# A two-layer graph network: the first layer's sums mapped to values head by head, and branch numbers loaded at other places

## The chip, the cores and the metric

The kernel runs on one core of one Trainium2 chip. The metric is the device time of one execution in microseconds (us). PE is TensorE (PEld its weight loads), DVE is VectorE, ACT is ScalarE, POOL is GpSimd, SP is SyncE. All data are float32.

## What is computed

6250 nodes with 160 features (64 scalars, 32 vectors of three components) and 200,000 edges, sorted by their target node `dst`, pass two message layers. Each layer starts with a layer norm and a relu. Cut to what matters:

```python
# layer 0, for every edge, H = 4 heads
msg = (norm(node) @ W_src)[src] + (norm(node) @ W_dst)[dst]
m1 = tensor_product(msg, y, rbf @ W_rbf)
a = leaky(m1_s @ W_alpha).reshape(e, H, 16) . alpha_dot           # one logit a head
ex = exp(a - segment_max(a, dst)[dst]);  den = segment_sum(ex, dst)
m2 = tensor_product(sigmoid(m1_s @ Ws_val), m1_v @ Wv_val * gate, y, w2)
h = concat(m2_s @ Ws_vlin, m2_v @ Wv_vlin)     # 16 + 24 values for each of 4 heads
out = node + segment_sum(ex / den * h, dst) @ Wp
# layer 1, for every edge
w = silu(rbf @ Wfc1) @ Wfc2
mid = w * tensor_product(f[src], y)            # 384 values
out = sc + alpha * (segment_mean(mid, dst) @ Wl2)
```

## The kernel before, in words

**Stages.** A short set-up and node stage; layer 0 over 391 groups of 512 edges (`layer0`); a node stage (`node1`); layer 1 over 392 groups (`layer1`); a last node stage (`node2`). In a layer the engines run their own instruction streams, coupled by semaphores, and loop over the groups with a hardware loop. The order of the work is written out by hand: `schedule` unrolls layer 0 by two groups, `by_fours` unrolls layer 1 by four. A step of layer 0 holds the start of group g (`now`), the middle of g-1 (`mid`) and the end of g-2 (`late`).

**The sums of layer 0.** The mapping to values is linear, so it is done after the sum over edges. For a group PE multiplies the 128 features of each of four blocks with the weights of each edge for (head, node slot), 4 x 32 columns: `sum_products` (L802), 16 matmuls of 128x128 into `sum_bank`, features on the partitions. ACT copies the bank to `held` (L902). `project` (L809) then maps features to values: 4 matmuls with `held` as the 128x128 stationary side and `w_val` as the moving side, whose columns are the values of all four heads (4 x 41 columns in the first block, 4 x 24 in the other three). The result has (head, slot) on the partitions and the values of all heads in its columns; of each partition only the 41 columns of its own head are used. `take_window` (L990) picks them with four DVE instructions, one for each head's 32 partitions, and `add_sums` (L998) adds them to the running sums with the factors of the running softmax. Then follow the peak of the next logits (L1095, L977 to L985) and the products (L1053 to L1057).

**More windows.** A group whose nodes span more than two blocks of 32 runs an inner loop (`more_of`), decided by a number that every engine loads from SBUF into a register (`value_load`). On PE in layer 0 this load comes behind `project` (`more_count`, L661). In layer 1 the number isn't there: PE and DVE load the first and the end count of a pair of groups (`more_of_pair`, L1339 and L1340) and compare them, and DVE loads the pair's row in `total` from `block_i` (L1658).

**Layer 1.** POOL gathers the source rows (L1497, 4 indirect DMAs a group, up to three groups ahead; the buffer of group g+3 is free when DVE has made the products of g-1). DVE makes one-hot rows (L1616) and products (L1625 to L1647), PE makes weights (L1527) and hidden inputs (L1516, L1517) and sums a window (L1538, 4 matmuls of 385 columns). In every second step DVE adds the pair's window to `total` with two instructions (`merge`, `add_window`, L1653).

## Time and profile before

| | |
|---|---|
| median of 3 runs | 8944.23 us (8936.49 to 8950.29) |
| the profiled execution | 8938.21 us |
| its span (first to last instruction) | 8936.4 us |
| PE / DVE / ACT / POOL busy | 89 / 82 / 37 / 67% of the span |
| mean granted TensorE clock | 0.929 of 2.4 GHz |

The profile lists instructions by source line and engine. A matmul of float32 data appears as two passes, each with its own weight load, so 4 matmuls are 8 records. Busy time is that of instructions on an engine's data path; register loads, branches and semaphore waits are not busy, and appear as idle time in front of the next instruction, with a name for what ended it ("issue" where the profile sees no releaser). A row `x1108 | 264.5, 239` means 1108 instructions, 264.5 us in total, 239 ns each.

### The profile page before, as it was taken

How to read it: one execution, taken by the hardware profiler on the slowest of the kernel's cores; microseconds unless marked ns; L12 is line 12 of the kernel's file. 1: busy time of each engine (PE TensorE's matmuls, PEld its weight loads, DVE VectorE, ACT ScalarE, POOL GpSimd, SP SyncE). 2: the span in 40 equal slices, each digit the busy share in tenths (PEclk: the TensorE clock that was granted, in tenths of full speed). 3: DMA queues.
4: the chain of work that ended last, by engine and by line, in shares of the span. 5: the costliest groups of instructions: out<-in, count | busy, mean ns of one | idle time of the engine just before them, and what ended most of it. 6: DMA issues, size and time to landing. Idle time of an engine off the chain costs nothing. (4 is left out here: it accounts for less than half of the span.)

```text
span 8936.4 us, 202775 instructions
## 1 busy us (share of the span) xinstructions
PE 7983.1 (89%) x50701; PEld 6094.9 (68%) x50702; DVE 7351.8 (82%) x18803; ACT 3272.5 (37%) x8375; POOL 5977.1 (67%) x5890
## 2 busy tenths in 40 slices
PE   2699999999999999999999999787968888888888
PEld 1488888888888888888888888666634444444445
DVE  4699999999999999999999999675368888887886
ACT  1244444444444444444444444332222222222223
POOL 0577777777777777777777777551046666666664
PEclk9799999999999999999999999898568888888888
DMA  3344444444444444444444433220012222222222
GB/s 54 78 99 99 98 98 99 98 99 98 99 98 99 98 98 99 99 98 99 98 99 98 99 98 98 66 70 23 11 43 65 64 65 65 64 65 64 65 64 58
DMA packets 616620, 725.49 MB, mean 81 GB/s; under 512 B 284132, under 2 KB 390884, under 8 KB 616573
## 3 DMA queue, kind: packets, MB, share of 16 engines
q0 software_dynamic: 225408, 385.00, 19.6%
q1 hardware_dynamic: 391165, 339.92, 15.0%
q8 instruction: 22, 0.36, 0.0%
q14 instruction: 25, 0.20, 0.0%
HBM read 708.40 MB, written 16.06 MB: 81 GB/s over the span
## 5 line engine op out<-in xcount | busy, mean ns | idle before, releaser
L720 POOL DMA_INDIRECT got_src<-src_tab,idx x1564 | 1773.3, 1134 | 659.3 <-POOL idx L714 358.4
L778 PE MATMUL bank_pair<-w_msg,blocks 128*128 128x160 f32 (+2 forms) x15640 | 2067.2, 288 | 61.3 <-DVE blocks L1030 61.3
L778 PEld LDWEIGHTS bank_pair<-w_msg,blocks 128*128 128x128 f32 x15640 | 1975.2, 192 | 100.3 <-DVE blocks L1030 95.5
L1497 POOL DMA_INDIRECT gotf<-f_tab,idx x1568 | 1536.2, 980 | 758.0 <-issue 466.2
L720 POOL DMA_INDIRECT got_dst<-dst_tab,idx x1564 | 1499.0, 958 | 529.3 <-issue 505.5
L802 PEld LDWEIGHTS bank_pair<-weights_t,product 128*128 128x128 f32 x12896 | 1496.5, 195 | 309.3 <-issue 294.9
L802 PE MATMUL bank_pair<-weights_t,product 128*128 128x128 f32 x12896 | 1573.3, 281 | 8.9 <-ACT weights_t L929 8.2
L1538 PE MATMUL bank_pair<-val,to_node 128*128 128x385 f32 x3136 | 1328.5, 573 | 2.7 <-DVE val L1647 2.7
L1589 ACT ACTIVATE val<-pre,y_edge 128x160 f32<-128x160 f32 x1568 | 542.7, 417 | 1618.6 <-DVE pre L1629 1614.7
L1538 PEld LDWEIGHTS bank_pair<-val,to_node 128*128 128x128 f32 x3136 | 658.1, 221 | 593.1 <-issue 348.7
L767 PE MATMUL bank_pair<-edge,w_edge 64*128 64x512 f32 x3128 | 884.8, 642 | 5.0 <-DVE blocks L1030 5.0
L936 ACT ACTIVATE rl<-bank_pair 128x256 f32<-128x256 f32 x391 | 150.2, 384 | 1801.9 <-PE bank_pair L778 1801.9
L1527 PE MATMUL bank_pair<-w_fc,hid 64*128 64x192 f32 x3136 | 399.1, 376 | 315.7 <-DVE val L1647 306.4
L897 ACT ACTIVATE product<-gated,y_edge 128x96 f32<-128x96 f32 x1564 | 458.1, 363 | 573.4 <-DVE gated L1134 573.2
L1527 PEld LDWEIGHTS bank_pair<-w_fc,hid 64*128 64x128 f32 x3136 | 272.7, 202 | 565.8 <-DVE val L1647 424.3
L737 POOL TENSOR_TENSOR edge<-rbf,y 128x512 f32<-128x512 f32 x391 | 500.8, 1281 | 234.6 <-PE bank_pair L778 227.5
L809 PEld LDWEIGHTS bank_pair<-w_val,held 128*128 128x128 f32 x3224 | 412.2, 190 | 307.2 <-ACT held L902 307.2
L730 POOL TENSOR_TENSOR msg<-got_src,got_dst 128x640 f32<-128x640 f32 x391 | 607.4, 1554 | 16.0 <-PE bank_pair L767 8.9
L990 DVE TENSOR_TENSOR win_scaled<-bank_pair,side 32x82 f32<-32x82 f32 x1612 | 384.8, 239 | 188.2 <-PE bank_pair L809 129.6
L1030 DVE TENSOR_TENSOR blocks<-bank_pair,turned_low 128x512 f32<-128x512 f32 x782 | 500.8, 680 | 32.5 <-PE bank_pair L767 28.1
L1030 DVE TENSOR_TENSOR blocks<-bank_pair,turned_high 128x512 f32<-128x512 f32 x782 | 502.1, 683 | 24.7 <-PE bank_pair L767 19.7
L1616 DVE TENSOR_TENSOR to_node<-iota_row,slot 128x512 f32<-128x512 f32 x392 | 270.6, 690 | 274.1 <-PE bank_pair L1538 141.7
(265 smaller groups left out, 12830.9 us busy)
## 6 DMA issues: line engine op xcount, KB each, us to landing
rbf<-in_rbf SPq DMA_DIRECT2D x391, 256.0 KB
dst_bc<-in_dst_rows SPq DMA_DIRECT2D x391, 256.0 KB
y<-in_y SPq DMA_DIRECT2D x391, 128.0 KB
y<-in_y SPq DMA_DIRECT2D x391, 96.0 KB
gotf<-f_tab,idx POOLq DMA_INDIRECT x1568
got_src<-src_tab,idx POOLq DMA_INDIRECT x1564
got_dst<-dst_tab,idx POOLq DMA_INDIRECT x1564
rbf<-in_rbf SPq DMA_DIRECT2D x392, 32.0 KB
```

What stands on the lines that cost most here:

```text
L720: pool.indirect_dma_start(out=buf[slot][:, t, :], out_offset=None, in_=table[:, :], in_offset=bass.IndirectOffsetOnAxis(ap=idx[slot][:, c: ...
L730: pool.tensor_tensor(msg[slot][:], got_src[slot][:], got_dst[slot][:], ALU.add).then_inc(s["summed"], 1)
L737: pool.tensor_tensor(edge[slot][:], rbf8[slot][:], y8[slot][:], ALU.mult).then_inc(s["scaled"], 1)
L767: nc.tensor.matmul(ebank[half], w_edge[r, pair, :], weigh.operand[r, :], start=True, stop=True).then_inc(s["weighed"], 1)
L778: return nc.tensor.matmul(to, blocks[rows, k, P * t:P * t + P], w_msg[rows, c0:c1], start=start, stop=stop)
L802: last = nc.tensor.matmul(sum_bank[:, P * b:P * b + P], product[slot][:, t, b, :], weights_t[:, t, :], start=t == 0, stop=t == TILES - 1)
L897: last = nc.scalar.activation(product[slot][:, t, 1:4, 64:96], gated[:, t, CS:D].rearrange("p (x c) -> p x c", x=3), ACT.Copy, scale=y_edg ...
L1030: dve.tensor_tensor(blocks[:, k, :], ebank[k % 2], (turned_low, turned_high)[k // 2][:], ALU.mult).then_inc(s["block_done"], 1)
L1497: pool.indirect_dma_start(out=got[k][:, t, :], out_offset=None, in_=f_tab[:, :], in_offset=bass.IndirectOffsetOnAxis(ap=idx[k][:, t:t + 1] ...
L1527: last = nc.tensor.matmul(weights[k % 2][:, t, 0:192], hid[k % 2][r, P * (t % 2):P * (t % 2) + P], K["w_fc2"][r, :], start=True, stop=True)
L1538: last = nc.tensor.matmul(win[k // 2], to_node[k % 2][:, t, :], val[k][:, t, :], start=k % 2 == 0 and t == 0, stop=k % 2 == 1 and t == TIL ...
L1589: last = nc.scalar.activation(val[k][:, t, 0:D], pre[:, t, 0:D], ACT.Copy, scale=y_edge[k][:, t, 0:1])
```

## The change

`project` is cut by heads. For each block b and head h one matmul takes the 32 columns of `held` that belong to h as stationary side and the 41 or 24 columns of `w_val` of that head as moving side, and writes 32 partitions. 4 matmuls become 16. The result `win` is 128 x 41, and `take_window` is one DVE instruction on 128 partitions. PE's number of further windows in layer 0 is loaded ahead of the wait for `held`. In layer 1 the row and the count of a pair are packed in one integer (`marks`, row + 64 x count); DVE loads it inside `products`, behind L1641, PE at the start of the step; `more_from` is loaded only where the count is above zero.

```diff
-        win = psum[3][:, 512:512 + HEADS * SB].rearrange("p (h c) -> p h c", h=HEADS)
+        win = psum[3][:, 512:512 + SB]
...
                 def project():
                     for b in range(4):
                         cols = slice(0, SB) if b == 0 else slice(AS, HV)
-                        last = nc.tensor.matmul(win[:, :, cols], held[:, P * b:P * b + P], w_val[:, b, :, cols],
-                                                start=b == 0, stop=b == 3)
+                        for h in range(HEADS):
+                            r = slice(BLK * h, BLK * h + BLK)
+                            last = nc.tensor.matmul(win[r, cols], held[:, P * b + BLK * h:P * b + BLK * h + BLK], w_val[:, b, h, cols],
+                                                    start=b == 0, stop=b == 3)
...
                     if late:
+                        count = more_count(pe, g - 2)
                         pe.wait_ge(s["sum_copied"], g - 1)
                         project().then_inc(s["projected"], 1)
...
-                        more_of(pe, g - 2, more_count(pe, g - 2), more)
+                        more_of(pe, g - 2, count, more)
...
                 def take_window(g):
-                    for h in range(HEADS):
-                        r = slice(BLK * h, BLK * h + BLK)
-                        last = dve.tensor_tensor(win_scaled[r, :, :], win[r, h, :].unsqueeze(1).broadcast_to([BLK, 2, SB]),
-                                                 side[r, at_group(g), :].rearrange("p a c -> p (a c)").unsqueeze(2).broadcast_to([BLK, 2, SB]),
-                                                 ALU.mult)
-                    return last
+                    return dve.tensor_tensor(win_scaled[:], win.unsqueeze(1).broadcast_to([P, 2, SB]),
+                                             side[:, at_group(g), :].rearrange("p a c -> p (a c)").unsqueeze(2).broadcast_to([P, 2, SB]),
+                                             ALU.mult)
...
-def more_of_pair(eng, more_from, q):
+def more_of_pair(eng, more_from, q, count, body):
 
-    return (eng.value_load(more_from[0:1, at_pair(q)], min_val=0, max_val=MAX_W),
-            eng.value_load(more_from[0:1, at_pair(q + 1)], min_val=0, max_val=MAX_W))
+    with eng.If(count > 0):
+        first = eng.value_load(more_from[0:1, at_pair(q)], min_val=0, max_val=MAX_W)
+        body(first, first + count)
...
+                    dve.tensor_copy(scan_b[:], marks[:])
                     chain.step(dve.tensor_copy(scan_a[:], span_i[:]))
+                    chain.step(dve.scalar_tensor_tensor(scan_b[:], scan_a[:], 64.0, scan_b[:], ALU.mult, ALU.add))
+                    chain.step(dve.tensor_copy(marks[:], scan_b[:]))
...
+        def mark_of(eng, q):
+            return eng.value_load(marks[0:1, at_pair(q)], min_val=0, max_val=2 ** 12 - 1)
...
                 def step(i, k):
                     g = i * 4 + k
...
+                    merging = k % 2 == 1 and not (fixed and g < 2)
+                    if merging:
+                        count = mark_of(pe, i * 2 + k // 2 - 1) >> 6
                     if not (fixed and g + 1 >= NG_PAD):
                         make_weights(i + (k + 1) // 4, (k + 1) % 4)
...
-                def products(i, k):
+                def products(i, k, merging):
...
+                    mark = mark_of(dve, i * 2 + k // 2 - 1) if merging else None
                     dve.wait_ge(s["along"], g * 3 + 2)
...
-                def merge(i, k, y0_done):
+                def merge(i, k, y0_done, mark):
                     q, half = i * 2 + k // 2, k // 2
-                    row = dve.value_load(block_i[0:1, at_pair(q)], min_val=0, max_val=NT - 1)
+                    row, count = nc.s_assert_within(mark & 63, 0, NT - 1), mark >> 6
                     dve.wait_ge(s["window_sum"], q * 2 + 2)
...
                     add_window(half, q, row).then_inc(s["merged"], 1)
-                    first, end = more_of_pair(dve, more_from, q)
-                    with dve.If(first < end):
+
+                    def body(first, end):
```

PE in the loop of layer 0, from the second pair of edge matmuls (L767) to the branch; L809 and L811 are `project`. Before:

```order
L767 MATMUL bank_pair<-edge,w_edge 128x512 x2
L809 MATMUL bank_pair<-w_val,held 128x164
L809 MATMUL bank_pair<-w_val,held 128x4x24 x3
L661 REGISTER_ALU
L661 TENSOR_LOAD marks
L661 ISA x2
L664 REGISTER_ALU
L664 COMPARE_AND_BRANCH
```

The same place of the changed kernel:

```order
L767 MATMUL bank_pair<-edge,w_edge 128x512 x2
L661 REGISTER_ALU
L661 TENSOR_LOAD marks
L661 ISA x2
L811 MATMUL bank_pair<-w_val,held 32x41 x4
L811 MATMUL bank_pair<-w_val,held 32x24 x12
L664 REGISTER_ALU
L664 COMPARE_AND_BRANCH
```

The load has moved ahead of `project`, and 4 matmuls are 16.

DVE in the loop of layer 1, a step with a merge, from the last product (L1647) to the branch over further windows. Before:

```order
L1647 TENSOR_TENSOR val<-along,bank_pair 128x4x32
L1658 ISA
L1658 TENSOR_LOAD block_i
L1658 ISA x2
L1659 ISA
L1653 ISA
L1653 SCALAR_TENSOR_TENSOR total<-bank_pair,here,total 128x385
L1653 ISA
L1653 SCALAR_TENSOR_TENSOR total<-bank_pair,after,total 128x385
L1339 REGISTER_ALU
L1339 TENSOR_LOAD more_from
L1339 ISA x2
...
```

The same place of the changed kernel, from one instruction group earlier; L1652 and L1659 are the lines L1641 and L1647 of before, L1666 is `add_window`:

```order
L1652 TENSOR_TENSOR val<-pre,y_edge 128x4x192
L1458 ISA
L1458 TENSOR_LOAD marks
L1458 ISA x2
L1656 REGISTER_ALU
L1657 TENSOR_TENSOR along<-along 128x4x32
L1658 REGISTER_ALU
L1659 TENSOR_TENSOR val<-along,bank_pair 128x4x32
L1671 REGISTER_ALU x2
L1671 ISA
L1672 ISA
L1666 ISA
...
```

One load stands behind the long product, and the loads of `block_i` (L1658 of before) and `more_from` are gone from between the last product and the next step: behind the second `add_window` only a register operation and the branch follow.

## Rows read from the trace of the kernel before

**Rows 1.** The page, part 2: TensorE's granted clock in 40 slices, in tenths.

```profile
PEclk9799999999999999999999999898568888888888
```

**Rows 2.** Engines by stretch, the steady parts of layer 0 and layer 1.

```profile
core 0: us, PE busy (x) PEld busy (x) DVE busy (x) ACT busy (x) POOL busy (x), PEclk, DMA share, GB/s
1000.00:5000.00 4000.00, 3878.09 (x28838) 3297.50 (x28838) 3640.01 (x9986) 1727.14 (x4161) 3145.25 (x3050) 1.00 0.41 98
6800.00:8800.00 2000.00, 1721.12 (x6913) 891.88 (x6912) 1610.78 (x3452) 569.86 (x1725) 1350.67 (x1382) 0.87 0.28 64
```

**Rows 3.** Who waited for whom in 1000 to 5000: us, times, longest.

```profile
PE bank_pair L796 <- ACT weights L948: 82.7, 181, 1.7
...
PE bank_pair L778 <- DVE blocks L1030: 30.1, 98, 0.4
```

**Rows 4.** Groups of instructions by line and shape, 1000 to 5000.

```profile
L720 POOL DMA_INDIRECT got_src<-src_tab,idx x1110 | 1270.6, 1145 | 468.2 <-POOL idx L714 255.0 <-issue 213.2
...
L720 POOL DMA_INDIRECT got_dst<-dst_tab,idx x1109 | 1055.5, 952 | 377.2 <-issue 359.6 <-PE bank_pair L767 17.7
...
L990 DVE TENSOR_TENSOR win_scaled<-bank_pair,side 32x82 f32<-32x82 f32 x1108 | 264.5, 239 | 42.3 <-issue 23.0
...
L809 PE MATMUL bank_pair<-w_val,held 128*128 128x96 f32 x1662 | 223.5, 268 | 0.0
...
L998 DVE SCALAR_TENSOR_TENSOR sums<-sums,factors,win_scaled 128x41 f32 x554 | 195.6, 392 | 62.9 <-DVE win_scaled L990 62.9
...
L796 PE MATMUL bank_pair<-ident,weights 128*128 128x128 f32 x1112 | 182.2, 286 | 91.8 <-ACT weights L948 82.7
```

**Rows 5.** Timeline, PE in one step of layer 0: start, us, what.

```profile
3011.35 3.84 PE L802 MATMUL bank_pair<-weights_t,product 128*128 128x128 f32 x32
...
3015.12 1.13 PE L767 MATMUL bank_pair<-edge,w_edge 64*128 64x512 f32 x4
...
3016.18 1.19 PE L809 MATMUL bank_pair<-w_val,held 128*128 128x164 f32 x8
...
3017.21 0.63 PE L791 MATMUL bank_pair<-ident,logits_wide 128*128 128x128 f32 x4
...
3017.67 4.39 PE L778 MATMUL bank_pair<-w_msg,blocks 128*128 128x160 f32 x34
```

**Rows 6.** Timeline, weight loads of 64 columns in layer 1.

```profile
7606.48 0.13 PEld L1516 LDWEIGHTS bank_pair<-rbf,w_fc 16*64 16x64 f32 x1 [0.22 <-issue]
...
7606.54 0.13 PEld L1516 LDWEIGHTS bank_pair<-rbf,w_fc 16*64 16x64 f32 x1
```

**Rows 7.** Timeline, DVE's products and POOL's gathers, two steps of layer 0.

```profile
3007.90 1.22 DVE L1053 TENSOR_TENSOR product<-gated,y_edge 128x1024 f32<-128x1024 f32 x1
...
3008.88 1.06 POOL L720 DMA_INDIRECT got_src<-src_tab,idx  x1 [0.30 <-issue]
...
3022.08 1.22 DVE L1053 TENSOR_TENSOR product<-gated,y_edge 128x1024 f32<-128x1024 f32 x1
...
3022.66 2.13 POOL L720 DMA_INDIRECT got_src<-src_tab,idx  x1 [0.30 <-issue]
```

**Rows 8.** Timeline, DVE from last product to next step, layer 1.

```profile
7845.88 0.29 DVE L1647 TENSOR_TENSOR val<-along,bank_pair 128x128 f32<-128x128 f32 x1
...
7846.92 0.62 DVE L1653 SCALAR_TENSOR_TENSOR total<-bank_pair,here,total 128x385 f32 x1 [0.76 <-PE bank_pair L1538]
...
7847.45 0.61 DVE L1653 SCALAR_TENSOR_TENSOR total<-bank_pair,after,total 128x385 f32 x1
...
7849.35 0.69 DVE L1616 TENSOR_TENSOR to_node<-iota_row,slot 128x512 f32<-128x512 f32 x1 [1.29 <-issue]
```

**Rows 9.** Groups of instructions by line and shape, 6800 to 8800.

```profile
L1497 POOL DMA_INDIRECT gotf<-f_tab,idx x1382 | 1350.9, 977 | 649.9 <-issue 410.6 <-DVE val L1647 239.3
```

**Rows 10.** Two stretches of layer 1, one at each clock (columns of rows 2).

```profile
7588.00:7597.80 9.80, 7.18 (x30) 3.72 (x28) 7.70 (x17) 3.30 (x10) 7.17 (x8) 1.00 0.29 67
7598.20:7604.90 6.70, 6.70 (x19) 3.67 (x20) 5.11 (x11) 1.65 (x5) 4.62 (x5) 0.50 0.28 59
```

More of the change, by code:

```diff
@@ L1359, in layer1 @@
         after = tmp("after", [P, PAIRS])
-        block_i = tmp("block_i", [1, PAIRS], I32)
+        marks = tmp("marks1", [1, PAIRS], I32)
         more_from = tmp("more_from", [1, PAIRS + 1], I32)
@@ L1385, in _ @@
                 def _(dve):
-                    chain = Chain(dve, s["step"], 25)
+                    chain = Chain(dve, s["step"], 27)
                     chain.begin(0)
@@ L1411, in _ @@
                     chain.step(dve.tensor_tensor(pair_row[:, 1, :], rows[:, 1, :, 0], rows[:, 1, :, 1], ALU.max))
[L1412 removed]
+                    dve.tensor_copy(marks[:], pair_row[:, 0, :])
                     chain.step(dve.tensor_tensor(scan_a[:], pair_row[:, 1, :], pair_row[:, 0, :], ALU.subtract))
[L1414 removed]
+                    dve.tensor_scalar(marks[:], marks[:], 7, None, ALU.logical_shift_right)
                     chain.step(dve.tensor_copy(span_i[:], scan_a[:]))
                     chain.step(dve.tensor_scalar(span_i[:], span_i[:], 7, None, ALU.logical_shift_right))
+                    dve.tensor_copy(scan_b[:], marks[:])
                     chain.step(dve.tensor_copy(scan_a[:], span_i[:]))
+                    chain.step(dve.scalar_tensor_tensor(scan_b[:], scan_a[:], 64.0, scan_b[:], ALU.mult, ALU.add))
+                    chain.step(dve.tensor_copy(marks[:], scan_b[:]))
                     a, b, d = scan_a, scan_b, 1
@@ L1540, in sum_window, with more_of @@
                     last.then_inc(s["window_sum"], 1)
-                def more_of(i, k):
+                def more_of(i, k, count):
                     q, half = i * 2 + k // 2, k // 2
-                    first, end = more_of_pair(pe, more_from, q)
-                    with pe.If(first < end):
+                    def body(first, end):
                         with pe.Fori(first, end) as w:
@@ L1552, in more_of @@
                             wait_apart(pe, s["more_added"], w + 1, s["tick_p"])
+                    more_of_pair(pe, more_from, q, count, body)
                 def step(i, k):
@@ L1567, in step @@
                         sum_window(i + (k + 3) // 4 - 1, (k + 3) % 4)
-                    if k % 2 == 1 and not (fixed and g < 2):
-                        more_of(i + (k + 2) // 4 - 1, (k + 2) % 4)
+                    if merging:
+                        more_of(i + (k + 2) // 4 - 1, (k + 2) % 4, count)
                     if fixed and g == NG_PAD - 1:
                         sum_window(i, k)
-                        more_of(i, k)
+                        more_of(i, k, mark_of(pe, i * 2 + k // 2) >> 6)
                 by_fours(step)(pe)
@@ L1647, in products @@
                     dve.tensor_tensor(val[k][:, :, D + 3 * CS:SUM], along[:, :, 0, :], w[:, :, 160:192], ALU.mult).then_inc(s["product"], 1)
+                    return mark
                 def add_window(half, q, row):
@@ L1662, in merge, with body @@
                     add_window(half, q, row).then_inc(s["merged"], 1)
-                    first, end = more_of_pair(dve, more_from, q)
-                    with dve.If(first < end):
+                    def body(first, end):
                         wait_apart(dve, s["merged"], q + 1, s["tick_v"])
@@ L1667, in merge @@
                             more(half, q, row, first, w, y0_done)
+                    more_of_pair(dve, more_from, q, count, body)
                 def more(half, q, row, first, w, y0_done):
@@ L1697, in step @@
                         make_hidden(0, 1)
-                    products(i, k)
-                    if k % 2 == 1 and not (fixed and g < 2):
-                        merge(i + (k + 2) // 4 - 1, (k + 2) % 4, g + 1)
+                    merging = k % 2 == 1 and not (fixed and g < 2)
+                    mark = products(i, k, merging)
+                    if merging:
+                        merge(i + (k + 2) // 4 - 1, (k + 2) % 4, g + 1, mark)
                     if fixed and g == NG_PAD - 1:
-                        merge(i, k, g + 1)
+                        merge(i, k, g + 1, mark_of(dve, i * 2 + k // 2))
                 by_fours(step)(dve)
```

2 lines of the change are left out of this document (removed).

## Prediction

> **What bounds the kernel now.** I read the clock line of the page first. TensorE has its full clock through layer 0 (slices 3 to 25) and loses about a fifth of it from slice 28 on [rows 1], so the two layers are two cases. The table by stretch then gives the load of each engine [rows 2].
>
> In layer 0, 277 groups (1108 instructions of L990, four a group) take 4000 us, 14.44 us a group. Three engines are close to their limits.
> - PE is busy 3878 of 4000 us. What it waits for is the end of DVE's work on the logits (L796, 91.8 us of idle time) and DVE's blocks (L778, 30.1 us) [rows 3, 4]: 122 us, 0.44 us a group. PE's own work is 14.0 us.
> - DVE is busy 3640 us, 13.1 us a group. The list of waits holds no row in which DVE waits for PE or ACT; its idle 1.3 us are register work and its own results. So DVE's own path is the whole 14.44 us, and PE follows it.
> - POOL is busy 3145 us and idle 468 + 377 us ahead of its gathers, together 3991 of 4000 us [rows 2, 4]. That idle time is almost all "issue" or its own index copy; only 17.7 us of it waits for PE. But POOL is elastic. The gather in front of which DVE has run L1053 for 0.98 us takes 1.06 us, the one that starts 0.58 us behind L1053 takes 2.13 us [rows 7]; the gathers of `got_src` take 1.145 us on average, those of `got_dst` 0.952 [rows 4]. It looks as if DVE's run of SBUF instructions (L1053 to L1057) holds such a gather back. With the four at 0.96 us each, like those of `got_dst`, POOL would need 14.4 - 4 x 0.18 = 13.7 us.
>
> In layer 1, 1382 gathers are 345 groups in 2000 us: 5.80 us a group, 11.6 a pair. PE is busy 86%, part of it at the low clock; DVE 81%; POOL is busy 1351 us, idle 411 us as issue and 239 us waiting for DVE's products [rows 2, 9], so its own pace is 5.1 us a group, 10.2 a pair. DVE sets the pace: between its last product and the next step lie 3.18 us, of which the two additions need 1.15; 0.76 us in front of them and 1.29 us behind them are idle [rows 8]. The first is named after PE, the second is issue. By the order of instructions one register load stands in the first place and two in the second.
>
> **take_window, DVE.** Four instructions of 239 ns leave, one of 128 partitions and the same 82 elements a partition comes [rows 4]. I price it at one of the four, 0.24 us. From below it can't be less; from above, if it took as long as all four do, nothing is saved. L998 works on 128 partitions with 41 elements in 392 ns, waits for POOL included; that would be the other plausible price. So DVE saves 0.72 us a group (0.56 to 0.72), and its path is 14.44 - 0.72 = 13.7 us.
>
> **project, PE.** 8 passes become 32. From L809 to L791 PE needs 3017.21 - 3016.18 = 1.03 us now [rows 5]. What a pass with 32 stationary and 41 or 24 moving columns costs, no row shows. The full passes of 128 columns cost 0.115 us (L791: 0.46 us for 4; L802: 3.77 us for 32) [rows 5]. Two weight loads of 64 columns follow each other after 0.06 us [rows 6], about half of that, so loading goes by columns, and 32 columns would be 0.03. Moving 41 columns at the rate of 128 in 0.115 is 0.037, 24 columns 0.022. With loads beside matmuls the longer of the two counts: 8 x 0.037 + 24 x 0.03 = 1.02 us. The bounds: no saving for size, 32 x 0.115 = 3.7 us; and four heads fully beside each other on four column strips, a quarter, 0.26 us. I take 1.02 us because the 64-column row is the nearest. L802's 32 passes leave 3.77 - 32 x 0.115 = 0.09 us ahead of L767, which works on another array shape; I add 0.1 us once, since PE now changes shape behind `project` too. Sum: 1.1 us against 1.03, +0.1 us on PE (-0.7 to +2.7).
>
> The Trainium skill, TensorEngine Tiling (Array Packing), section Instruction Overhead, says that a matmul has about 60 cycles of overhead on this chip, so that one with a single column lasts as long as one with 60; an estimate from that page is 25 ns a pass and 0.8 us for the 32, and the forecast would stay. No row here has so short a pass.
>
> The number of further windows is loaded ahead of the wait for `held`, while PE's array still works on L767, which lasts 1.06 us up to L809 [rows 5]. One such load costs DVE 0.76 us at most [rows 8]. So it is hidden; without that cover it would cost up to 0.76 us. Behind `project` a load less stands in front of L791; L791 follows at once today, so nothing is gained.
>
> **Layer 0.** DVE's path 13.7, PE's work 14.0 + 0.1 = 14.1 with no wait left, POOL between 13.7 and 14.4. Some of PE's work now overlaps its waits, so 14.1 is rather high; POOL will still be hit by some of DVE's runs. I take 14.05 (13.85 to 14.25): 0.39 us x 391 groups = 152 us gained (74 to 230).
>
> **The loads of layer 1, DVE.** The load of a pair's row moves behind L1641, an instruction of 0.95 us that was issued before it, and costs nothing while it is shorter than that; if not, up to 0.1 us in L1645. The idle 0.76 us shrinks to waits and address arithmetic, say 0.15: -0.6. The 1.29 us lose two loads; branch and loop remain, say 0.4: -0.9. DVE's pair falls by 1.5 us (1.2 to 1.7) to 10.1. What is late next is POOL at 10.2, and PE at the low clock (0.50 of 2.4 GHz, so 1.2): in that stretch PE is busy 6.70 of 6.70 us and DVE waits, in the fast one, at 2.4 GHz, it is busy 7.18 of 9.80 [rows 10]. A slow stretch of 6.7 us takes 3.4 us of work from PE. Today PE's idle time of 14% [rows 2] and DVE's slow way take most of it up. With 1.5 us less a pair, and a slow stretch in every second pair as now, I estimate that half of the 3.4 us reaches DVE, 0.8 us a pair. If the clock stays as it is, the pair ends near 10.1 + 0.8 = 10.9; if PE, which waits less, keeps its clock, near POOL's 10.2. I take the middle, 10.55: 1.0 us x 196 pairs = 200 us gained (135 to 270). PE's own load stands where PE waits for DVE's products anyway. Four more instructions in the set-up are under 1.5 us, once. POOL and SP issue what they did.
>
> **Sum.** 8938.2 - 152 - 200 + 1 = 8587 us against the profiled execution's own time; the median is 6 us above that: 8593. Own range 8500 to 8690.
>
> **Rivals.**
> 1. POOL is the bound of layer 0. For it: 3991 of 4000 us are accounted for without a wait. Against: the 2.13 us gather shows that it is stretched, not loaded. Then layer 0 stays and only layer 1 gains: 8944 - 200 = 8744.
> 2. Layer 1 hardly gains, since the slow spells of PE eat it (pair 11.3): 8944 - 152 - 60 = 8732.
> 3. `project` becomes the bound of layer 0, the slower side. If a pass costs the shortest full pass less the saving of moving columns, 0.085 us, it takes 2.8 us, PE's work is 14.0 + 1.8 = 15.8, and layer 0 loses 1.35 x 391 = 530 us: 8944 + 530 - 200 = 9270. For it: each pass is still a load and a matmul. Against: the 64-column row. It decides from the point where PE's work exceeds 14.44 + 200/391 = 14.95 us, that is +0.95 us or 59 ns a pass.
> 4. A pass costs what L1516's load costs, 0.06 us, whatever its size: 32 x 0.06 + 0.1 = 2.0 us, PE's work 15.0, layer 0 loses 0.55 x 391 = 215 us, and layer 1 gives it back: 8944 + 215 - 200 = 8959, or up to 100 us less if PE's waits already overlap its work. The Trainium skill, TensorE: Matmul & The Clock Gate, section Wait — 56ns, not 53.3ns?, names about 62 ns per MATMUL in one mode of the sequencer as a bound for short matmuls; no row here shows it.
>
> **Chances.** Forecast 0.48; rival 1 0.17; rival 2 0.13; rival 4 0.10; rival 3 0.09; the remaining 0.03 faster still, if strips run beside each other. A difference under 0.2% (18 us) can't be told from none. Faster: 0.48 + 0.17 + 0.13 + 0.03 + half of rival 4 = 0.86; within 0.2% 0.03; slower 0.11. The range for 8 in 10 is 8450 to 8850: it holds rivals 1 and 2, and leaves rival 3 and the most of 4 out.
>
> **What the profile of the changed kernel would show.** L991 once a group with about 0.24 us. `project` from its first pass to L791 in 1.1 us; 1.9 us or more means rival 3 or 4, and PE without idle time in layer 0. A period of 14.05 us a group; if it is 14.4 with the sum of POOL unchanged, rival 1. No wait of PE for ACT's weights at L796. In layer 1 no idle time over 0.3 us ahead of `add_window`, and POOL's wait for DVE's products near nothing; a mean clock above 0.87 there says that the slow spells became fewer, one below that speaks for rival 2. The prediction is wrong if the span of layer 0 grows, or if the pair of layer 1 stays over 11.2 us.

## The result and the profile after

The changed kernel takes 8687.08 us (median of 4 runs, 8681.67 to 8747.73); the kernel before, timed on the same chip, 8940.36. The ratio is 0.973, with a 95% interval of 0.969 to 0.978: 253 us less. The forecast was 8590 (8450 to 8850), so 350 less: right in sign and range, too large by 97 us. One of the four executions of a later run, `strip_third`, took 8849 us, 2.7% above the median of its others, and is left out of its ratio.

By the first and the last of GpSimd's message additions (L730) in the two traces, layer 0 lasts from 322 to 5978 us (before: 322 to 6141), and 2702.2 us follow (before: 2795.6). So layer 0 gave 163 us where 152 were forecast, and the rest 93 where 200 were. The clock line and the engines by stretch (line 1 layer 0, line 2 layer 1) answer to [rows 1, 2]:

```profile
PEclk9799999999999999999999999987569999999999
```

```profile
core 0: us, PE busy (x) PEld busy (x) DVE busy (x) ACT busy (x) POOL busy (x), PEclk, DMA share, GB/s
1000.00:5000.00 4000.00, 3833.32 (x36377) 3197.39 (x36375) 3688.62 (x9385) 1755.23 (x4264) 3124.61 (x3127) 1.00 0.42 101
6800.00:8600.00 1800.00, 1487.40 (x6458) 781.66 (x6456) 1517.83 (x3234) 533.40 (x1616) 1405.76 (x1295) 0.94 0.29 67
```

In layer 1 the granted clock rises from 0.87 to 0.94, and GpSimd's busy share from 68% to 78%. The groups of layer 0 by line and shape, which answer to [rows 4]; each has its total, its mean in ns and the idle time in front of it:

```profile
L720 POOL DMA_INDIRECT got_src<-src_tab,idx x1137 | 1205.1, 1060 | 479.8 <-POOL idx L714 261.5 <-issue 212.8 <-PE bank_pair L767 5.5
L720 POOL DMA_INDIRECT got_dst<-dst_tab,idx x1137 | 1080.1, 950 | 385.2 <-issue 366.9 <-PE bank_pair L767 18.3
...
L730 POOL TENSOR_TENSOR msg<-got_src,got_dst 128x640 f32<-128x640 f32 x284 | 440.6, 1551 | 4.9
...
L998 DVE SCALAR_TENSOR_TENSOR sums<-sums,factors,win_scaled 128x41 f32 x570 | 354.7, 661 | 66.4 <-DVE win_scaled L991 66.4
...
L1095 DVE CUSTOM_DVE_ANT_0 near<-bank_pair,far 128x512 f32<-128x512 f32 x285 | 193.5, 679 | 6.7 <-issue 6.7
...
L796 PE MATMUL bank_pair<-ident,weights 128*128 128x128 f32 x1136 | 186.5, 287 | 10.0 <-ACT weights L951 8.7
...
L811 PE MATMUL bank_pair<-w_val,held 128*32 128x24 f32 x6816 | 102.6, 188 | 0.0
...
L991 DVE TENSOR_TENSOR win_scaled<-bank_pair,side 128x82 f32<-128x82 f32 x284 | 67.8, 239 | 34.3 <-issue 26.4
```

L991 takes 239 ns on 128 partitions, as on 32, and PE's wait at L796 has all but gone (10.0 us where it was 91.8). The line that stands out is L998: the same two instructions a group take 661 ns on average where they took 392. The timeline of one step (start, duration) shows them and `project`:

```profile
3007.95 0.46 PE L811 MATMUL bank_pair<-w_val,held 128*32 128x41 f32 x32
...
3008.65 0.63 PE L791 MATMUL bank_pair<-ident,logits_wide 128*128 128x128 f32 x4 [0.23 <-issue]
...
3009.78 0.23 DVE L991 TENSOR_TENSOR win_scaled<-bank_pair,side 128x82 f32<-128x82 f32 x1
...
3010.01 1.55 POOL L730 TENSOR_TENSOR msg<-got_src,got_dst 128x640 f32<-128x640 f32 x1
3010.24 1.56 DVE L998 SCALAR_TENSOR_TENSOR sums<-sums,factors,win_scaled 128x41 f32 x2 [0.23 <-DVE win_scaled L991]
```

`project` from its first pass to L791 is 0.70 us with 32 passes, against 1.03 with 8 [rows 5]. The two additions, 1.56 us together, end just behind GpSimd's addition of the messages. The means hide two kinds of addition, as the shortest, the median and the longest of L998 show (ns):

```profile
L998 DVE SCALAR_TENSOR_TENSOR sums<-sums,factors,win_scaled x570: 246/263/1397, 999.0 to 4997.4; 128x41 f32 x190
```

One that nothing disturbs takes 0.25 us, and in the step above the first takes 1.39 us and the second 0.25. In layer 1 the gathers (to be held against [rows 9]), the waits for them, and the two additions of a pair:

```profile
L1504 POOL DMA_INDIRECT gotf<-f_tab,idx x1295 | 1407.3, 1087 | 394.5 <-issue 394.5
...
L1636 DVE TENSOR_TENSOR pre<-bank_pair,gotf 128x512 f32<-128x512 f32 x324 | 223.9, 691 | 199.5 <-DMA gotf<-f_tab,idx 197.7 <-issue 1.1
...
L1666 DVE SCALAR_TENSOR_TENSOR total<-bank_pair,here,total 128x385 f32 x162 | 100.3, 619 | 43.9 <-issue 43.9
```

VectorE's idle time in front of `add_window` is 0.27 us a pair on average, where it was 0.76 in [rows 8]. GpSimd no longer waits for VectorE at all, its gathers are 1.087 us instead of 0.977, and VectorE has a wait for gathered rows.

### The profile page after: what moved, and what is told of

Same layout as the page of the kernel before. It is cut to its first block and busy times, and to the rows that moved or that the text cites. A ratio compares the mean times of both kernels' runs of the same rounds, so it can differ in the third digit from the quotient of the medians.

```text
span 8679.9 us, 218293 instructions
## 1 busy us (share of the span) xinstructions
PE 7627.6 (88%) x60373; PEld 5771.5 (66%) x60374; DVE 7274.4 (84%) x17597; ACT 3252.4 (37%) x8375; POOL 6016.9 (69%) x5890
## 5 line engine op out<-in xcount | busy, mean ns | idle before, releaser
L720 POOL DMA_INDIRECT got_src<-src_tab,idx x1564 | 1661.5, 1062 | 659.4 <-POOL idx L714 358.5
L1504 POOL DMA_INDIRECT gotf<-f_tab,idx x1568 | 1702.3, 1086 | 514.2 <-issue 477.4
L1545 PE MATMUL bank_pair<-val,to_node 128*128 128x385 f32 x3136 | 1247.6, 545 | 5.0 <-DVE val L1659 5.0
L1545 PEld LDWEIGHTS bank_pair<-val,to_node 128*128 128x128 f32 x3136 | 621.6, 208 | 536.8 <-issue 270.1
L767 PE MATMUL bank_pair<-edge,w_edge 64*128 64x512 f32 x3128 | 884.8, 642 | 9.5 <-DVE blocks L1030 9.5
L1534 PE MATMUL bank_pair<-w_fc,hid 64*128 64x192 f32 x3136 | 363.1, 349 | 378.8 <-DVE val L1659 378.6
L1534 PEld LDWEIGHTS bank_pair<-w_fc,hid 64*128 64x128 f32 x3136 | 252.0, 187 | 615.0 <-issue 335.5
L737 POOL TENSOR_TENSOR edge<-rbf,y 128x512 f32<-128x512 f32 x391 | 500.5, 1280 | 199.4 <-PE bank_pair L778 192.2
L730 POOL TENSOR_TENSOR msg<-got_src,got_dst 128x640 f32<-128x640 f32 x391 | 606.5, 1551 | 14.0 <-PE bank_pair L767 7.2
L998 DVE SCALAR_TENSOR_TENSOR sums<-sums,factors,win_scaled 128x41 f32 x806 | 477.7, 632 | 92.9 <-DVE win_scaled L991 92.6
L1053 DVE TENSOR_TENSOR product<-gated,y_edge 128x1024 f32<-128x1024 f32 x391 | 476.4, 1219 | 0.0
L1636 DVE TENSOR_TENSOR pre<-bank_pair,gotf 128x512 f32<-128x512 f32 x392 | 270.9, 691 | 242.8 <-DMA gotf<-f_tab,idx 240.8
```

Source lines behind the costliest of these rows:

```text
L720: pool.indirect_dma_start(out=buf[slot][:, t, :], out_offset=None, in_=table[:, :], in_offset=bass.IndirectOffsetOnAxis(ap=idx[slot][:, c: ...
L730: pool.tensor_tensor(msg[slot][:], got_src[slot][:], got_dst[slot][:], ALU.add).then_inc(s["summed"], 1)
L737: pool.tensor_tensor(edge[slot][:], rbf8[slot][:], y8[slot][:], ALU.mult).then_inc(s["scaled"], 1)
L767: nc.tensor.matmul(ebank[half], w_edge[r, pair, :], weigh.operand[r, :], start=True, stop=True).then_inc(s["weighed"], 1)
L998: last = dve.scalar_tensor_tensor(to, to, factors[:, n:n + 1], win_scaled[:, n, :], ALU.mult, ALU.add)
L1504: pool.indirect_dma_start(out=got[k][:, t, :], out_offset=None, in_=f_tab[:, :], in_offset=bass.IndirectOffsetOnAxis(ap=idx[k][:, t:t + 1] ...
```

## The experiments

All are timed beside the kernel before on the same chip; the ratio is to that. The kernel before took 8930 to 8940 us in these timings (but for the last run), so differences of 10 or 20 us between runs show nothing. Each is the changed kernel with the edit named. The period is layer 0's, the mean distance of GpSimd's message additions (L730) from 1000 to 5000 us; the pair is layer 1's, the mean time of two steps.

**One layer at a time.** `l0_only` has the edits of layer 0, `l1_only` those of layer 1 (the diff above, split between its two functions).

> Only the edits of layer 0 (project head by head, one take_window, PE's count loaded earlier); layer 1 as before. The traces give a period of 14.08 us a group against 14.43, 0.35 x 391 = 137 us. Theory A (the two layers' gains are independent and add up): 8940 - 140 = 8800 us, layer 1 pair 11.58 us. Rival (part of layer 0's gain is only in the stages around it, or layer 1 gained by a different clock history): 8850 or more, or 8700 to 8750.

> Only the edits of layer 1 (packed marks, loads at other places); layer 0 as before. Theory A: the pair falls from 11.58 to 11.13 us, 0.45 x 196 = 88 us: 8850 us, and POOL's gathers in layer 1 take 1.09 us as in the changed kernel, since it is DVE's denser work in layer 1 that stretches them. Rival: gathers of 0.98 us and a pair near 10.6, about 8750 us, if something from layer 0 (code, buffers, clock) stretched them.

Measured: `l0_only` 8723.7 (ratio 0.977 [0.976, 0.979], 207 us less than before), period 14.04, pair 11.38. `l1_only` 8851.6 (0.992 [0.990, 0.993], 79 us less than before), period 14.42, pair 11.12. So layer 1's edits are worth 0.45 us a pair, not 1.0. The sum of both, 286, is 33 more than the two together bring: `l0_only`'s layer 1, whose code is the old one, was also 0.2 us a pair quicker (11.58 before), 54 us behind the last message in the traces. So `l0_only` misses its own theory's 8800 and falls into the rival's range, but not for the rival's reason: the granted clock from 6700 to 8500 us was 0.87 to 0.88, as before. Why is open.

**The window's product in four pieces again, `project` left cheap** (`four_windows`):

```
-    return dve.tensor_tensor(win_scaled[:], win..., side[:, ...], ALU.mult)
+    for h in range(HEADS):
+        r = slice(BLK * h, BLK * h + BLK)
+        last = dve.tensor_tensor(win_scaled[r, :, :], win[r, :]..., side[r, ...], ALU.mult)
+    return last
```

> The changed kernel, but take_window is again four DVE instructions of 32 partitions each, from the smaller result. Theory A (DVE's path is what set layer 0's pace): the 0.75 us come back on DVE, the period returns to about 14.4 us a group, 8687 + 130 = 8820 us. Rival B (PE's shorter project made the gain): the period stays at 14.1 and the time at 8690 us. Rival C (POOL is the bound): between, 8690 to 8750 us.

Measured: 8854.6 (0.992 [0.990, 0.993]), period 14.42. Its groups of layer 0:

```profile
L993 DVE TENSOR_TENSOR win_scaled<-bank_pair,side 32x82 f32<-32x82 f32 x1108 | 264.8, 239 | 43.8 <-issue 24.0
...
L1001 DVE SCALAR_TENSOR_TENSOR sums<-sums,factors,win_scaled 128x41 f32 x554 | 194.9, 390 | 62.9 <-DVE win_scaled L993 62.9
```

The time is that of `l1_only`: of layer 0's gain nothing is left, although `project` is the short one. Layer 0's gain comes from VectorE's instructions alone, and VectorE is what paced layer 0 before. The longer time of L998 (L1001 here) comes with their going.

**`project` with the head as the outer loop** (`one_strip`). A matmul here is two passes, so eight passes in a row use the same strip of columns, where it were two.

```
-                    for b in range(4):
-                        cols = slice(0, SB) if b == 0 else slice(AS, HV)
-                        for h in range(HEADS):
+                    for h in range(HEADS):
+                        for b in range(4):
+                            cols = slice(0, SB) if b == 0 else slice(AS, HV)
```

> The changed kernel with project's loops swapped: the four matmuls of one head follow each other in one column strip, then the next head. Theory S (the passes are cheap, 0.46 us for 32, because neighbours run on different column strips): project takes 1.0 us or more instead of 0.46, and since PE is not the bound by 0.3 us a group the time rises by 0 to 60 us, 8687 to 8750. Rival L (a pass costs what its 32 columns cost, whichever strip): project stays at 0.46 us and the time at 8687.

Measured: 8646.2 (0.968 [0.966, 0.970]). The step is longer, though a little short of the 1.0 us expected: 0.93 us from the first pass to L791 against 0.70, and this row stands against L811 above:

```profile
3009.96 0.94 PE L811 MATMUL bank_pair<-w_val,held 128*32 128x41 f32 x32
```

So passes on different strips do run beside each other. The starts of the single passes say the same: in the changed kernel four passes, one on each strip, start 7 ns apart, and the next four 32 ns behind them once the row is under way; in `one_strip` the passes of a strip also start 32 ns apart, one after the other, and the next strip starts only 165 ns behind the one before it. The time came out 41 us less than the changed kernel's, where 0 to 60 more was expected; the intervals of the two ratios, 0.966 to 0.970 and 0.969 to 0.978, overlap. A later pair of runs takes that back: `act_third` and `strip_third` (below) differ in this loop alone and take 8617.9 and 8621.0. And the profiled executions show that layer 0 can go in more than one way with the same code. `act_third` has the changed kernel's layer 0, and its period is 15.45 us in groups 3 to 42, 14.46 in the next forty, 13.98 from there to 5000 us; `one_strip` has 15.46, 14.46 and 13.95, while the changed kernel and `strip_third` go at 14.05 to 14.2 in all of these and at 14.07 from 1000 to 5000 us. So nothing shows that the 41 us are the loop's. What makes a run go the one way or the other stays open.

**A product of layer 1 with one operand from PSUM** (`psum_operand`):

```
 dve.tensor_tensor(val[k][:, :, D:D + 3 * CS]...,
-                  o[:, :, D:D + CS].unsqueeze(2)...,          # pre, in SBUF
+                  w[:, :, CS:2 * CS].unsqueeze(2)...,         # the weights, in PSUM
                   y.broadcast_to(...), ALU.mult)
```

> The changed kernel with one operand exchanged: the product of three vector parts in layer 1 (VectorE, L1652) takes the weights of its second third, which lie in PSUM, where it took the source's part, which lies in SBUF. So 192 of an edge's products lack the source's factor; the instruction keeps its shape, type and count, but one of its inputs no longer comes from SBUF. Layer 0 is not touched. Theory P (VectorE's instructions with two SBUF inputs hold up the GpSimd gathers of layer 1, which end about 0.3 us after L1650 or L1657 end): with the longest of them gone the mean gather falls from 1.086 to about 1.0 us or less, the pair of steps from 11.13 to 10.4 to 10.8 us (8 gathers by 0.08 to 0.09, that is 0.6 to 0.7 us), 190 pairs: 8550 to 8620 us. Rival B (the gathers are longer because more transfers or more of VectorE's work in general lies beside them): gather 1.08, pair 11.1, 8670 to 8700 us. Rival C: the instruction with a PSUM input is itself slower, VectorE becomes the bound and the pair grows: 8700 to 8800 us.

Measured: 8548.3 (0.957 [0.956, 0.959]), 139 us less than the changed kernel. VectorE's line is as long as before (L1652, 0.95 us); GpSimd's is not:

```profile
L1504 POOL DMA_INDIRECT gotf<-f_tab,idx x1248 | 1257.2, 1007 | 380.5 <-issue 380.5
```

The gather falls from 1.087 to 1.007 us, the pair to 10.51. The profiled execution (8521 us) has 2584 us behind the last message, 118 less than the changed kernel's 2702; its other 43 us are nearly all in layer 0, whose code is the same and which here ran at 13.97 from 1000 to 5000 us. Theory P holds, B and C fall: the traffic rose from 67 to 71 GB/s while the gathers got shorter, so what makes them long is where VectorE's second operand lies. The granted clock rose as well, from 0.94 to 0.98, but GpSimd still waits for nothing, and its own 8 x (1.007 + 0.305) = 10.5 us are the pair. The product is by another operand here, so this run is a probe and no kernel to use.

**ScalarE makes a third of that product** (`act_third`):

```
+    nc.scalar.activation(val[k][:, t, D:D + CS], pre[:, t, D:D + CS], ACT.Copy, scale=y_edge[k][:, t, 1:2])
-    dve.tensor_tensor(val[k][:, :, D:D + 3 * CS] ...
+    dve.tensor_tensor(val[k][:, :, D + CS:D + 3 * CS] ...    # two parts instead of three
```

> The changed kernel with one of the three vector parts of the product in layer 1 moved from VectorE (L1652, 768 elements a step, now 512) to ScalarE (two more instructions a step by a tile's scale, for which PE's window sums wait as for the old ones). The result is the reference's. Theory P (two-input runs of VectorE hold up the gathers): L1652 falls from 1.10 to about 0.75 us, the lock is 0.3 us a step shorter, the gather mean falls from 1.086 to about 1.04, the pair from 11.13 to 10.7 to 10.95: 8630 to 8665 us. Rival B (nothing to do with VectorE's runs): 11.1, 8680 us. Rival D (ScalarE's added 0.25 to 0.5 us a step lies ahead of the window sums and the step grows): pair 11.2 to 11.6, 8700 to 8770 us.

Measured: 8617.9 (0.964 [0.962, 0.966]), 69 us less than the changed kernel; gather 1.049 us, pair 10.84, and 2644 us behind the last message, 58 less. Of the kernels that compute everything it is the quickest, together with `strip_third` (below), which can't be told from it. (ScalarE got four more instructions a step, one a tile, not the two that the expectation has.)

**No copy of the window sum** (`sums_psum`), layer 0: VectorE scales the sums in place and adds the window sum from PSUM.

```
-  take_window(g - 2).then_inc(s["win_scaled"], 1)
+  for n in range(2):
+      last = dve.tensor_scalar(tos[n], tos[n], factors[:, n:n + 1], None, ALU.mult)
+  last.then_inc(s["win_scaled"], 1)
-  add_sums(b).then_inc(s["merged"], 1)
+  for n in range(2):
+      last = dve.scalar_tensor_tensor(tos[n], win, sides[:, n:n + 1], tos[n], ALU.mult, ALU.add)
+  last.then_inc(s["merged"], 1)
```

> The changed kernel, in layer 0 alone: the copy of the window sum from PSUM (L991) is left out of the groups' loop, the sums are scaled in place by two instructions with a scalar, and the two additions read the window sum from PSUM, so no VectorE instruction of the step has two SBUF inputs. Same number of VectorE instructions plus one; PE waits for the sums, 0.5 us later than for the copy. The result is the reference's. Theory P (L998 grew from 392 to 661 ns because GpSimd's addition of the messages holds the port that a two-input VectorE instruction needs): the two additions take 0.3 to 0.4 us each again, GpSimd's later work starts earlier, period 14.08 falls to 13.7 to 13.95 (-50 to -150 us): 8540 to 8640 us. Rival B (the length of L998 has nothing to do with the port, or GpSimd's own sum of 13.7 plus issue binds): additions 0.6 us again or period 14.05 to 14.1, 8670 to 8700 us. Rival W (PE waits for the sums at L830): period 14.2 to 14.6, 8730 to 8850 us.

Measured: 9014.9 (1.0095 [1.008, 1.011]), slower than before the change; period 14.98. The groups say why:

```profile
L1089 DVE TENSOR_SCALAR sums<-sums,factors x534 | 452.5, 888 | 37.4 <-issue 37.4
...
L1093 DVE SCALAR_TENSOR_TENSOR sums<-bank_pair,side,sums 128x41 f32 x534 | 114.2, 255 | 25.2 <-DVE sums L1089 20.4
```

and the same place in its timeline, GpSimd first, then VectorE:

```profile
3013.50 1.55 POOL L730 TENSOR_TENSOR msg<-got_src,got_dst 128x640 f32<-128x640 f32 x1
```

```profile
3013.27 1.99 DVE L1089 TENSOR_SCALAR sums<-sums,factors  x2
3015.41 0.43 DVE L1093 SCALAR_TENSOR_TENSOR sums<-bank_pair,side,sums 128x41 f32 x2 [0.15 <-DVE sums L1089]
```

and the shortest, the median and the longest of each (ns):

```profile
L1089 DVE TENSOR_SCALAR sums<-sums,factors x534: 228/244/1842, 1004.1 to 4990.0; - x178
L1093 DVE SCALAR_TENSOR_TENSOR sums<-bank_pair,side,sums x534: 248/256/265, 1005.9 to 4990.5; 128x41 f32 x178
```

The additions with PSUM in place of one SBUF input never take more than 265 ns, as theory P said; but the scaling, one input in SBUF and a scalar, now takes the wait: 1.84 us for the first in the step above, which meets GpSimd's addition, and 0.23 for the second, 0.89 on average. None of the three theories had that.

**One gather of eight left out** (`seven_gathers`), layer 0: `if t == TILES - 1 and buf is got_dst: continue`.

> The changed kernel, in layer 0 alone: one of the eight gathers of a group (the destination rows of the fourth tile) is left out after the first two groups, so the messages of that tile are made from rows that stand there from before. GpSimd loses one gather a group (0.95 us and 0.3 us of issue). Theory G (GpSimd, which has no idle time in the steady part of layer 0, sets the period of 14.08 us): the period falls until the next engine binds, PE at 13.7 or VectorE's chain, 285 groups by 0.3 to 0.4: 8570 to 8610 us. Rival V (the period is set by the chain VectorE blocks to PE and back, and GpSimd's work stretches to fill it): period 14.0 to 14.08, 8660 to 8690 us.

Measured: 8618.4 (0.966 [0.963, 0.969]), period 13.88. GpSimd loses 1.25 us of 14.07 and the period follows for 0.2 of it; the gathers of `got_src` stretch to 1.264 us, and VectorE and GpSimd now wait for PE (L769, which is L767 above: 52 and 56 us). So GpSimd holds layer 0 up by 0.2 us a group at most, and against the 13.97 at which `psum_operand` ran the same layer 0, by 0.1. That is between G and V: several engines are within 0.2 us of each other.

**ScalarE scales the sums** (`sums_act`), so that VectorE has only the two additions that read PSUM:

```
+  b, _, _ = marks_of(act, g - 1)
+  for n in range(2):
+      to = sums[:, bass.ds(b + n, 1), :]...
+      last = nc.scalar.activation(to, to, ACT.Copy, scale=factors[:, n:n + 1])
```

> The changed kernel, in layer 0 alone: ScalarE scales the two rows of sums in place (two activations by the factor, after the weights' copy, with a branch number of its own), VectorE's copy of the window sum (L991) is gone, and its two additions read the window sum from PSUM. So of the run of 2 us on VectorE (0.23 copy, 0.23 wait, 1.56 two additions) about 0.45 us stays, and none of it has two SBUF inputs or one in the form that took 0.89 us in sums_psum. The result is the reference's. Theory P (the additions were long because GpSimd's message addition holds the port): additions 0.25 us each as in sums_psum, VectorE's busy time per group falls by 1.3 us, period from 14.08 to 13.8 (GpSimd at 13.9 in seven_gathers, PE at 13.7): 290 groups by 0.15 to 0.35: 8590 to 8650 us. Rival R (the time comes back: the freed VectorE runs into the gathers at other places, or ScalarE's branch number and two additions delay the weights or the scalars' gates that PE and VectorE wait for): period 14.1 to 14.6: 8690 to 8830 us.

Measured: 8712.3 (0.975 [0.973, 0.977]), 25 us more than the changed kernel; period 14.21. Five groups of it, the additions once more with their shortest, median and longest:

```profile
L1143 DVE TENSOR_TENSOR gated<-vec,gates 128x384 f32<-128x384 f32 x281 | 388.7, 1383 | 9.7
...
L1104 DVE CUSTOM_DVE_ANT_0 near<-bank_pair,far 128x512 f32<-128x512 f32 x282 | 195.0, 692 | 82.3 <-issue 77.1
...
L1096 DVE SCALAR_TENSOR_TENSOR sums<-bank_pair,side,sums 128x41 f32 x564 | 135.1, 255 | 47.8 <-issue 46.6
...
L1075 DVE TENSOR_SCALAR far<-dst_bc,ring 128x512 f32<-128x512 int32 x282 | 195.3, 692 | 0.0
...
L1036 DVE TENSOR_TENSOR blocks<-bank_pair,turned_high 128x512 f32<-128x512 f32 x564 | 361.0, 680 | 65.4 <-PE bank_pair L767 65.4
...
L1096 DVE SCALAR_TENSOR_TENSOR sums<-bank_pair,side,sums x564: 239/259/264, 1003.9 to 4997.2; 128x41 f32 x188
```

and one step, the additions on VectorE and GpSimd's beside them:

```profile
3020.88 0.52 DVE L1096 SCALAR_TENSOR_TENSOR sums<-bank_pair,side,sums 128x41 f32 x2
```

```profile
3021.06 1.55 POOL L730 TENSOR_TENSOR msg<-got_src,got_dst 128x640 f32<-128x640 f32 x1
```

The two additions take 0.52 us although GpSimd's runs beside the second, and fell by 0.81 us a group; with L991 and the wait behind it gone, VectorE has 1.19 us less in this place. More than that came back, and the period grew by 0.13 us: 0.46 at `gated` (924 ns in the changed kernel, 1383 here), which has two SBUF inputs and now meets GpSimd's other `tensor_tensor` (L737, 1.28 us); 0.27 as issue ahead of `near`; 0.17 at L1075 (519 ns there) and 0.18 at the first of the small sums (251 ns there, 429 here); and 0.23 as a wait for PE's L767 ahead of L1036, which the changed kernel has not. That is rival R, for the most part by its first half; the wait for PE may belong to its second, and no run here parts the two.

**Edits together.** `strip_third` is `one_strip` with `act_third`, `all_three` adds `sums_act`.

> The changed kernel with two edits of earlier runs together: the maps to values with the head as the outer loop (layer 0, 41 us less alone) and ScalarE's third of the vector product (layer 1, 69 us less alone). They touch different layers, so additive: 8687 - 41 - 69 = 8577 us, 8560 to 8600. If the phase that one_strip's groups settle in is a matter of chance, 8600 to 8630. The result is the reference's.

> sums_act and strip_third together; the result is the reference's. If sums_act and the head as the outer loop work on the same thing (phase of VectorE's two-input work against GpSimd), they don't add: min of both in layer 0, and 69 us in layer 1: 8540 to 8580 us. If they add: 8500 to 8540 us. If sums_act is slower by itself, so is this: over 8600 us.

Measured: 8621.0 (0.964 [0.962, 0.966]) and 8680.1 (0.971 [0.969, 0.973]). The first (8609 to 8627 without the one of 8849) has layer 0 at 14.07 and 2649 us behind it: `act_third`'s gain and nothing of `one_strip`'s, the case for which the expectation gave 8600 to 8630. The second is `sums_act`'s layer 0 with `act_third`'s layer 1.

**Two thirds on ScalarE** (`act_two_thirds`):

```
+    for x in range(2):
+        last = nc.scalar.activation(val[k][:, t, D + x * CS:D + x * CS + CS], pre[:, t, D:D + CS], ACT.Copy, scale=...)
+    dve.tensor_tensor(val[k][:, :, D + 2 * CS:D + 3 * CS], o[:, :, D:D + CS], y_edge[k][:, :, 3:4]..., ALU.mult)
```

> act_third taken one part further: ScalarE makes two of the three vector parts (twelve instructions a step with the four by the first factor, 4.3 us by act_third's 0.417 and 0.333 us each, and 0.36 us of tanh, of a step of 5.4 us), VectorE's L1652 has 256 elements left. The result is the reference's. Theory P goes by the time for which a VectorE run with two SBUF inputs stands in a gather's way: another 0.27 us of it gone a step, gather mean from 1.049 to about 1.01, the pair of steps from 10.84 to 10.55 to 10.7, 30 to 55 us less than act_third's 8618: 8565 to 8590 us. Rival A (ScalarE's chain of 4.3 us behind L1640 now ends last ahead of the window sums, idle time of PE at L1545 behind ScalarE): pair 10.9 to 11.6, 8620 to 8750 us.

Inconclusive. The kernel before, timed beside it, took 10194 us, against 8930 to 8940 beside all others, and this one 10041 (0.985 [0.982, 0.988]); layer 0, whose code is the changed kernel's, had a period of 16.2 us, and PE 409.7 us of idle time ahead of `project`, where the changed kernel has none. What was different there I can't say, and nothing of it can be carried over to 8618.

## Why the prediction was right, and where it was not

**take_window.** Right: once a group, 239 ns, the size that I took. 0.72 us was the forecast; with the idle time in front of the four the two traces give (264.5 + 42.3) / 277 - (67.8 + 34.3) / 284 = 1.108 - 0.360 = 0.75.

**Layer 0, from 0.72 to 0.39.** The number came out (period 14.07, forecast 14.05) and `four_windows` shows that it is VectorE's instructions that bring it, but the way there was another, and that the two agree so closely is luck. I took VectorE's path as 13.7 and let PE, at 14.1, be the next bound. PE was not: its work fell to 3833 / 284 = 13.5 us. VectorE got back less than it gave. Counted from the groups of both traces, a group has 0.75 us less at `take_window`, 0.55 more at L998 with the wait ahead of it, 0.09 more in the first of the small sums behind `near`, and 0.19 less at `near`, probably because its registers are now made ready under L998: 0.30 less in all, of a period that fell by 0.35. That L998's growth is GpSimd's message addition in its way is shown by three things: of the pair in the step above the first, which runs into it, takes 1.39 us and the second, behind it, 0.25; with a PSUM input none takes more than 264 ns, with that addition beside them (`sums_act`); and in `sums_psum` and `sums_act` another instruction takes over the wait. So it is not the place of the operands by itself that costs, it is meeting GpSimd with two SBUF inputs. The Trainium skill, SBUF — State Buffer, section Who interferes with whom, has such a rule: VectorE and GpSimd share one pair of ports, and a VectorE instruction with two SBUF inputs gets in the way of a GpSimd instruction that reads SBUF, as a `tensor_scalar` in its two-port mode does of any; the one that comes second waits until the first is through. The traces agree: 1.39 and 1.84 us for the one that meets L730, against 0.25 and 0.23. Whether the `tensor_scalar` of `sums_psum` was in that mode no row shows.

**project.** Mis-sized: -0.33 us instead of +0.1. The 0.03 us a load fits one strip, where the passes start 32 ns apart; the wrong step was to add up all 32 of them one after the other, though four strips run beside each other. 32 passes that change the strip after every second take 0.46 us in the row above, those that change it after every eighth 0.94, in the same count and shapes; my lower bound, 0.26 us for fully parallel heads, was the nearer end: the last of the 32 starts 0.27 us behind the first. The 0.8 us for the 32 that the prediction sets beside its own sum is too much as well. It had no weight in the time, since PE is not what VectorE waits for (`four_windows`). Rivals 3 and 4, which made each pass cost 0.06 to 0.085 us, fall with it. A new idle time of 0.23 us, issue, stands between `project` and L791. By the times of the sequencer it belongs to the branch over further windows, which stood behind `project` before too (times of its instructions as shortest, median and longest, ns):

```profile
L664 PEldq COMPARE_BRANCH  x284: 208/208/208, 1011.0 to 4994.6; - x142
```

The branch takes 0.21 us of PE's sequencer, and from its start to L791's first pass it is 0.47 us on average in `one_strip` and in the changed kernel, and 0.48 in the kernel before. What differs is when it starts behind the first pass: 0.56 us before, 0.46 in `one_strip`, 0.23 in the changed kernel. So the 1.03 us that I priced as eight passes were the issue of the passes and the branch behind them, and with the short `project` the branch is no longer covered by passes under way.

**Rival 1**, GpSimd as layer 0's bound, falls: with the same instructions of GpSimd the period went from 14.43 to 14.07. GpSimd's busy and idle time again fill 3990 of 4000 us, as before; its gathers of `got_src` only stretch less, 1.060 us where it was 1.145. `seven_gathers` shows what is true in it, 0.1 to 0.2 us a group.

**Layer 1.** This is where the 97 us are. VectorE's share went as forecast: of the two idle times of 0.76 and 1.29 us around `add_window` [rows 8], 0.27 are left in front and 0.18 behind (28.9 us of waits for PE over 162 pairs), none in the step below, and GpSimd's wait for VectorE went from 239 us to nothing. One step of the changed kernel, VectorE and then GpSimd:

```profile
7602.53 0.94 DVE L1652 TENSOR_TENSOR val<-pre,y_edge 128x768 f32<-128x768 f32 x1
...
7603.40 0.28 DVE L1657 TENSOR_TENSOR along<-along 128x128 f32<-128x128 f32 x1
...
7604.25 0.62 DVE L1666 SCALAR_TENSOR_TENSOR total<-bank_pair,here,total 128x385 f32 x1 [0.25 <-issue]
...
7604.79 0.61 DVE L1666 SCALAR_TENSOR_TENSOR total<-bank_pair,after,total 128x385 f32 x1
7605.33 0.69 DVE L1627 TENSOR_TENSOR to_node<-iota_row,slot 128x512 f32<-128x512 f32 x1
```

```profile
7602.73 1.56 POOL L1504 DMA_INDIRECT gotf<-f_tab,idx  x1 [0.30 <-issue]
```

The gather that starts within VectorE's L1652 takes 1.56 us. The clock rose above 0.87, so rival 2's cause, the slow spells, did not eat the gain. The step that failed is "POOL at 10.2": I took GpSimd's pace from gathers of 0.977 us and 0.3 of issue. With VectorE's products following each other without a gap the gathers became 1.087, and 8 x (1.087 + 0.305) = 11.1 us is the pair, as measured (11.13). In layer 0 I had read the same stretching from [rows 7] and used it; in layer 1 I did not ask what VectorE's denser work would do to it. `psum_operand` shows it: one operand out of SBUF, gather 1.007, pair 10.51, which is the forecast's 10.55. `act_third` shows the same in a smaller dose.

The prediction called itself wrong if the pair stayed over 11.2 us; at 11.13 it passed that by 0.07 us. Layer 1 brought 93 us of the 200 forecast for it.

## What to carry to other kernels

Where VectorE and GpSimd are both near their limits, count besides the instructions those that meet at their common port: VectorE's with two SBUF inputs (or a scalar form in and out of SBUF) against GpSimd's reads. A saved microsecond on one of them comes back there in part, and an edit that moves such an instruction moves the wait to the next. Reading one operand from PSUM (`psum_operand`), or giving ScalarE a part of the product (`act_third`), took most or part of it away in layer 1; in layer 0 the same kind of edit moved it to other instructions (`sums_psum`, `sums_act`). And an edit of 0.5% must be judged by more than one pair of runs: the same layer settled at 13.97 or at 14.07 us a group.

## What the runs showed of the hardware

- 32 FP32 passes with 32 stationary columns each are through in 0.46 us where the column strip changes after every second pass, and in 0.94 where it changes after every eighth; the next transpose starts 0.70 and 0.93 us behind the first pass, of which 0.47 us runs from the start of the branch between them. Passes on four strips start 7 ns apart, passes on one strip 32 ns. The Trainium skill, TensorEngine Tiling (Array Packing), section Key Properties, says that tiles can load and multiply in parallel; both rows bear it out.
- `scalar_tensor_tensor` on 128 x 41 elements: 255 ns with one input in PSUM, whether GpSimd works beside it or not; 0.25 us with both in SBUF where nothing is in the way, and 1.39 us where it starts 0.23 us behind the start of a GpSimd addition of 1.55 us. `tensor_scalar` of the same size, SBUF to SBUF: 0.23 us and, beside that addition, 1.84. An average of 392, 661 or 888 ns is a mixture of the two.
- A branch on a register takes 0.21 us of PE's sequencer (L664).
- An indirect gather on GpSimd takes 0.95 us undisturbed, up to 2.13 beside VectorE's run L1053 to L1057 [rows 7], 1.087 on average in layer 1 beside VectorE's products of two SBUF inputs (L1644 to L1657), and 1.007 where one operand of the longest lies in PSUM.
